# Summing squares over 1024 hidden values: eight thin matmuls in place of seven GpSimd adds and one matmul

## The reference

```python
gu = jnp.einsum('bsd,hd->bsh', x, wq_gu)         # 256 -> 2048
gate, up = jnp.split(gu, 2, axis=-1)
h = jax.nn.silu(gate) * up                       # 1024 hidden values per token
hn = rms_norm(h)                                 # h * rsqrt(mean(h*h) + eps), per token
return jnp.einsum('bsh,dh->bsd', hn, wq_p)       # 1024 -> 256
```

## Time and profile before

| | us |
|---|---|
| median of 3 runs | 5025.49 |
| lowest and highest of them | 5015.09, 5025.96 |
| the profiled execution | 5015.09 |
| its span, from the first to the last instruction | 5013.3 |
| L3307, sums of squares, 32 MATMUL records, busy | 3.8 |
| L3314, output products, 256 records, busy | 56.2 |
| L3297, gate and up, 384 records, busy | 85.5 |
| L3327, 28 adds on GpSimd, busy | 35.5 |

### The profile page before, as it was taken

How to read it: one execution, slowest core, us unless ns; L and a number is a source line. 1 busy time by engine, 2 the same in 40 slices (tenths; PEclk the granted TensorE clock), 3 DMA queues, 4 the chain that set the end, 5 groups by cost and what they waited for, 6 DMA issues and landing times. The chain is left out here.

```text
span 5013.3 us, 110619 instructions
## 1 busy us (share of the span) xinstructions
PE 4262.7 (85%) x45600; PEld 2578.4 (51%) x45600; DVE 2255.0 (45%) x3826; ACT 1794.9 (36%) x2794; POOL 1186.7 (24%) x1661
## 2 busy tenths in 40 slices
PE   6789869999967858779898778988998988989869
PEld 3233744544543634446466655555555555555546
DVE  5932244334343251440422255555555565555631
ACT  2067122221220113230101255555555555555532
POOL 2000110000015141210000044444444444444412
PEclk9689679999988977889898688999889999899979
DMA  1000000000021510000100000000000000000000
GB/s 44 1 1 1 27 33 0 9 9 0 3 87 35 185 60 0 0 22 1 51 0 5 6 10 8 8 8 9 7 8 8 8 8 8 8 8 8 5 15 17
DMA packets 37869, 91.93 MB, mean 18 GB/s; under 512 B 6914, under 2 KB 27173, under 8 KB 33920
## 3 DMA queue, kind: packets, MB, share of 16 engines
q1 hardware_dynamic: 27072, 69.45, 4.0%
q0 software_dynamic: 6144, 11.62, 0.8%
q10 hardware_dynamic: 4224, 4.19, 0.3%
HBM read 69.96 MB, written 20.45 MB: 18 GB/s over the span
## 5 line engine op out<-in xcount | busy, mean ns | idle before, releaser
L2426 PE MATMUL ps<-h_normT,h_w 128*128 128x512 f32 (+1 forms) x1008 | 453.7, 557 | 61.6 <-DVE h_xx L3001 54.8
L2943 DVE SCALAR_TENSOR_TENSOR h_cv<-h_raw,h_cw,h_cv 128x1023 f32<-128x1023 f32 (+2 forms) x288 | 372.5, 1303 | 21.4 <-ACT h_cv L2776 18.6
L3062 DVE SCALAR_TENSOR_TENSOR h_st<-h_st,d_gcs,ps 128x64 f32<-128x64 f32 x448 | 125.0, 279 | 493.9 <-PE ps L2701 493.3
L2775 ACT ACTIVATE h_raw<-ps 128x512 f32<-128x512 f32 x192 | 114.8, 598 | 528.8 <-PE ps L2426 527.9
L2343 POOL TENSOR_TENSOR h_sq<-h_sq,h_qsq 128x512 f32<-128x512 f32 x64 | 79.9, 1269 | 809.6 <-ACT h_sq L2922 809.6
L2335 POOL TENSOR_TENSOR h_gm<-h_gm,h_tmp 128x15 f32<-128x15 f32 (+7 forms) x480 | 260.5, 543 | 37.6
L877 PE MATMUL ps<-a_probT,a_v 128*128 128x512 f32 x512 | 231.0, 611 | 25.3 <-DVE a_probT L939 25.3
L2426 PEld LDWEIGHTS ps<-h_normT,h_w 128*128 128x128 f32 x1008 | 172.2, 201 | 154.7 <-issue 135.6
L854 PE MATMUL ps<-a_qkT 128*128 128x512 f32 x512 | 230.1, 594 | 3.1 <-DVE a_v L930 3.1
L2701 PEld LDWEIGHTS ps<-h_st,h_mT 64*64 64x64 f32 x1792 | 93.6, 137 | 247.4 <-issue 241.4
L2334 POOL TENSOR_TENSOR h_tmp<-h_gm 128x15 f32<-128x15 f32 (+7 forms) x480 | 179.0, 373 | 128.9 <-DVE h_gm L2988 93.7
(11 more groups left out here) (517 smaller groups left out, 9535.7 us busy)
## 6 DMA issues: line engine op xcount, KB each, us to landing
m_wgu<-in_m_wgu SPq DMA_DIRECT2D x8, 1408.0 KB
h_w<-in_d_w SPq DMA_DIRECT2D x48, 128.0 KB, 2.1
m_wd<-in_m_wd SPq DMA_DIRECT2D x8, 704.0 KB
m_rows_in<-r_zero SPq DMA_DIRECT2D x4, 1024.0 KB, 13.3
e_xe<-m_rows_in SPq DMA_DIRECT2D x8, 512.0 KB
m_rows_out<-e_y ACTq DMA_DIRECT2D x8, 512.0 KB, 11.2
e_wgu<-in_e_wgu SPq DMA_DIRECT2D x1, 3520.0 KB
a_t_raw<-in_t_w SPq DMA_DIRECT2D x4, 768.0 KB, 4.4
```

What stands on the lines that cost most here:

```text
L2426: last = pe.matmul(ps[:, PROJ[m], lo:hi], w[:, kind, k, :], hT[:, k, b * S + tb * BANK + lo:b * S + tb * BANK + hi], start=(k == 0), stop= ...
L2943: dve.scalar_tensor_tensor(out=d, in0=raw[:, kind, 0:S - back], scalar=tap(pr, kind, TAPS3 - 1 - back), in1=d, op0=ALU.mult, op1=ALU.add). ...
```

## The change

GpSimd's part of `mlp3` goes, with its buffer `total` and its semaphore `added`. TensorE now takes each of the 8 squared tiles itself: for each of the 4 groups of tokens, 8 matmuls with one column of ones add up in PSUM. TensorE waits for the 8 squares of the block instead of the 7 adds; ScalarE waits for `ssum` before it writes over a square.

```diff
-        total = ph.sb("total", [P, 2, BANK])
...
-                    pe.wait_ge(added, tb * (MC3 - 1))
+                    pe.wait_ge(sq_r, tb * MC3)
                     if q >= 1:
                         pe.wait_ge(std_r, q)
                     for j in range(4):
-                        last = pe.matmul(ps[:, 4, j:j + 1], total[:, q % 2, j * P:(j + 1) * P], core.ones[:, 0:1], start=True, stop=True)
+                        for m in range(MC3):
+                            last = pe.matmul(ps[:, 4, j:j + 1], sq[:, q % 2, m, j * P:(j + 1) * P], core.ones[:, 0:1],
+                                             start=(m == 0), stop=(m == MC3 - 1))
                     last.then_inc(ssum, 1)
...
-        @block.gpsimd
-        def _(pool):
-            for tb in range(NTB):
-                for m in range(1, MC3):
-                    pool.wait_ge(sq_r, tb * MC3 + m + 1)
...
-                    pool.tensor_tensor(total[:, tb % 2, :], total[:, tb % 2, :] if m > 1 else sq[:, tb % 2, 0, :], sq[:, tb % 2, m, :],
-                                       ALU.add).then_inc(added, 1)
...
                 if tb >= 2:
-                    act.wait_ge(added, (tb - 1) * (MC3 - 1))
+                    act.wait_ge(ssum, tb - 1)
```

More of the change, by code:

```diff
@@ L3279, in mlp3 @@
         silu, hid, sq = ph.sb("silu", [P, 3, BANK]), ph.sb("hid", [P, 2, MC3, BANK]), ph.sb("sq", [P, 2, MC3, BANK])
-        total = ph.sb("total", [P, 2, BANK])
         std, rinv = ph.sb("std", [P, NT]), ph.sb("rinv", [P, NT])
-        gu, silu_r, hid_r, sq_r, added, ssum, std_r, rinv_r, out_p, x_added = (
-            ph.sem(n) for n in ("gu", "silu", "hid", "sq", "added", "ssum", "std", "rinv", "out", "x"))
+        gu, silu_r, hid_r, sq_r, ssum, std_r, rinv_r, out_p, x_added = (
+            ph.sem(n) for n in ("gu", "silu", "hid", "sq", "ssum", "std", "rinv", "out", "x"))
         block = ph.block()
```

## The result

The changed kernel took 5065.79 us (median of 4 runs, 5057.12 to 5071.15), the kernel before 5025.73 us in the same comparison (median of 4, 5015.09 to 5029.07). The ratio is 1.0084 with a 95% interval of 1.0059 to 1.0107: 40 us slower. The forecast was 5063 us, slower.

The account below looks back on a forecast made before the run. TensorE was taken to bound the last stage from end to end. Loads of 24.4 us plus clock falls of 16.4 us gave 40.8 us, 5055.9 on the profiled execution; forecast 5063 us, range 5045 to 5077.

Parts of the forecast that it names:

- What leaves is worth 0: Last stage: removing 28 adds from GpSimd, an engine with slack, gains 0.
- The waits are free: Last stage: moved waits of TensorE and ScalarE cost 0, with over 10 us of cover for the last square.
- 224 loads at 109 ns, 24.4 us: TensorE, last stage: 224 added fp32 records, each priced as a tile load, cost 24.4 us (22.2 to 26.0).
- The clock, 16.4 us: TensorE, last stage: the clock falls in each of four 7.0 us thin runs, 4.1 us each (total 0 to 25.6).
- The sum, 40.8 us: Whole kernel: loads of 24.4 us plus clock falls of 16.4 us, added to the profiled execution's 5015.1 us.
- Rival A: Last stage: the clock holds, so loads alone cost 24.4 us; 5050 us on the median; chance 0.14.
- Rival B: Output runs: the clock returns late, falls cost 42 us, not 16.4; 5092 us on the median; chance 0.07.
- Rival C: Sums at L3307: thin records nearly free, 3.1 us for 224; 5029 us on the median; chance 0.03.
- Rival D: Last stage: squares come late and TensorE waits, some us if in the last block only; chance 0.02.
- The base: Whole kernel: 5063 us set between 5055.9 on the profiled execution and 5066.3 on the median, which is 10.4 us higher.
- the prediction's own signs of being wrong: Profile after: off-pace L3307, clock 1.00 throughout, TensorE waiting for ScalarE, or earlier stages moving over 10 us.

Follow-up runs that it names:

- one_tile: The changed kernel with TensorE summing only the first of the 8 squared tiles and no adds on GpSimd; last stage 144.23 us.
- left4: Against the changed kernel, GpSimd adds the 8 tiles down to 4 and TensorE sums those, 32 records in a run; last stage 163.38 us.
- groups: The changed kernel with the first three blocks' thin matmuls issued four at a time behind the next block's gate/up products; last stage 170.67 us, median 5065.52 us.
- after_again: The changed kernel, code unchanged, timed again with more rounds on one chip; 1.0077 of the kernel before, last stage 190.83 us.
- left2: Against the changed kernel, GpSimd adds the 8 tiles down to 2 and TensorE sums those, 16 records in a run; last stage 147.81 us.
- the bf16 run: The changed kernel with the squares and the column of ones in bf16, each run of sums done once; last stage 144.47 us.
- bf16x8: The changed kernel with squares and column of ones in bf16 and each run of sums done eight times; last stage 177.66 us.
- spread_fp32: The changed kernel with its fp32 sums issued one at a time between wide matmuls instead of in a run; last stage 160.94 us.
- groups_again: The kernel with sums in groups of four, timed again with more rounds; 1.0046 of the kernel before, last stage 170.63 us.

## Why the prediction was right

- *What leaves is worth 0.* Shown by one_tile, 144.23 us against 144.54.
- *The waits are free.* No idle time of TensorE stands before the sums, after as before. ScalarE's root waited for the sums 46.0 us in 4 pieces (12.3 in one before) and nobody paid.
- *224 loads at 109 ns, 24.4 us.* It was 24.1. Taking the time at half clock out, a run of 64 records is 6.85 us, 107 ns a record; left4's undisturbed block says 108. The row that I took as nearest, 27 records in 3.00 us at full clock, was 4% high: at the measured pace 28 records fit in that stretch, not 27. The 99 ns of the short run was the lower end it was taken for: groups pays it again and again.
- *The clock, 16.4 us.* It was 18.8. Each of the four falls came. They came 5.1, 4.4, 2.2 and 5.3 us into the run, so r, the thin work left, was on average 2.6 us (I took 2.25); and from the first output matmul the clock needed 3.1, 5.4, 4.5 and 3.7 us to rise, on average 4.2 (I took 3.7). r + 4.2 / 2 = 4.7 us a fall. This is the one term that was sized a little low, and that it came so near is in part luck: 2.25 was the middle between a fall as early as the rows show and none inside the run, and no row stood behind that middle. Three of the four falls came later than the 2.5 to 3.5 us of the rows, and the earliest left 4.7 us of thin work and cost 6.8 us, over the 6.4 I had as the upper end. Two output runs grew by more than the 2.2 us that I gave as the most (2.7 and 2.3). The term also differs by execution: in after_again the stretches at half clock sum to 44.4 us, 22.2 us of cost, with the same 24.1 us of loads.
- *The sum, 40.8 us.* The stage gave 42.9, the medians 40.1. Rival A (the clock holds) would have been 24; it is wrong for the 6.9 us runs and right for the 1.7 us runs of left2 and for small groups. Rival B (no quick return) is wrong with 13.92 us of wide work behind each run. Rival C (nearly free) is wrong for fp32, at 107 ns a record; the bf16 run shows it can be had with another type. Rival D (late squares) saw no wait at all.
- *The base.* This was the weakest part of the figure, and luck helped it: 5063 was put between two bases 10.4 us apart, and of the changed kernel eight runs are on record, from 5050.41 to 5078.01 us, with a median of 5069.33; the four that were compared give 5065.79. One of the prediction's own signs of being wrong did come, a shift of more than 10 us before the stage: it is 14.8 us. Where the stage starts late in the profile after, L575 already starts at 569.7 us against 561.7, L1134 at 1488.6 against 1477.6, L1810 at 2239.7 against 2225.1: in stages whose instructions are the same. The clock there accounts for it. Summed from the granted clock in stretches of 2 us, TensorE was busy at half clock for 909 us before the last stage in the profile before and for 944 in the one after; half of the difference is 17 us. one_tile (GpSimd's part gone) and left2 (most of it kept) agree: 922 and 985 us, half of the difference is 31 us, and their last stages start at 4865.38 and 4896.66, 31.3 us apart. So the late start is clock lost in unchanged stages, by an amount that differs between executions. Why it differs stays open, and so does what makes the last stage start some 40 us later than the clock accounts for on the slower chip, that of bf16x8, spread_fp32, after_again and groups_again.

## What to carry to other kernels

Price a thin matmul (one or a few columns) by a measured row of the same tile and type and not by its columns, here 214 ns for an fp32 tile and 25 ns for a bf16 one in a row, and then look at how many stand in a row: a long row can also lose TensorE its clock (all of 6.9 us and three of four of 3.5 us did here, those of 1.7 us did not), and part of the bill comes on the wide matmuls behind it, with TensorE busy all the time. Work that another engine does in its slack was free here, and pulling it onto the engine that sets the end cost its whole price there. If it must be there, put it in small groups between wide work (16.7 us of 42.9 came back in the stage) or in bf16 (all 42.9 came back in one profile; the squares are then rounded). No version tried was shown to be faster than the kernel before. Compare variants of one stage by that stage's length in the profile when the other stages scatter by more than the effect.

## What the runs showed of the hardware

- The fall of the clock needs no idle time and no fp32: it came with 4.70 of 4.70 us busy, at 25 ns a bf16 record. The first row is the run, the second the fall:

```profile
4953.80:4958.50 4.70, 4.70 (x195) 4.70 (x192) 0.69 (x1) 2.40 (x3) 0.00 (x0) 1.00 0.01 3
4958.50:4959.00 0.50, 0.50 (x27) 0.50 (x24) 0.00 (x0) 0.00 (x0) 0.00 (x0) 0.93 0.00 0
```

- A bf16 thin matmul with a 128x128 tile takes 24 to 25 ns packed, less than an eighth of the 214 ns of the fp32 one. The lengths of the records don't say so: the load lasts 96 ns in its record (192 ns in fp32), and the records overlap. The columns are the shortest, the median and the longest duration in ns, the first and last start.

```profile
L3314 PEld LDWEIGHTS ps<-g_onesb,g_sq x128: 95/96/98, 4923.2 to 5009.7; 128*128 128x128 bf16 x128
L3314 PE MATMUL ps<-g_onesb,g_sq x128: 163/163/167, 4923.5 to 5009.8; 128*128 128x1 bf16 x128
```

  The Trainium skill has two statements that bear on this, which I had not used. TensorE: Matmul & The Clock Gate, section Weight-path perf modes, says that a fast weight load is on for 128 weights of a type other than fp32; 25 ns in bf16 against 107 ns a record in fp32 fits it. The same page, section Wait — 56ns, not 53.3ns?, says that matmuls don't start closer than about 25 ns however few their columns; the 24.4 and 24.8 ns of these runs stand at that figure. No run separates the two.
- The clock can fall after the thin run has ended, 1.1 us after it in left4, so a profile that shows wide matmuls at half clock may have its cause a microsecond earlier.
